# Attention as 64-row head pairs, with scores that telescope over key tiles

## What is computed

```python
h = _layernorm(x) * (1 + ca) + sa
qkv = (h @ W_qkv + b_qkv).reshape(b, l, 16, 192).transpose(0, 2, 1, 3)
Q, K, V = jnp.split(qkv, 3, axis=-1)
scores = einsum('bhqd,bhkd->bhqk', Q, K) / sqrt(64)
out = einsum('bhqk,bhkv->bhqv', softmax(scores), V)
x = x + ga * (out.transpose(0, 2, 1, 3).reshape(b, l, 1024) @ W_fc + b_fc)
```

## Time and profile before

| | |
|---|---|
| median of three runs | 1919.35 us (1916.85 to 1920.01) |
| the profiled execution's own time | 1920.44 us |
| its span, first to last instruction | 1918.7 us |
| mean granted TensorE clock | 0.971 |
| busy: PE, PEld, DVE, ACT, POOL | 1813.9, 991.3, 1313.7, 1051.4, 1169.5 us |
| instructions | 29207 |

### The profile page before, as it was taken

The page is one execution under the profiler, slowest core; times in us unless marked ns, Lnnn a source line. Parts: engine busy times, 40 slices in busy tenths (PEclk is TensorE's granted clock), DMA queues, the critical chain, the costliest instruction groups (busy, mean ns, idle before and its releaser), DMA issues. The chain is left out here.

```text
span 1918.7 us, 29207 instructions
## 1 busy us (share of the span) xinstructions
PE 1813.9 (95%) x7819; PEld 991.3 (52%) x7819; DVE 1313.7 (68%) x2687; ACT 1051.4 (55%) x1944; POOL 1169.5 (61%) x521
## 2 busy tenths in 40 slices
PE   4799999999999999999999999999999999946996
PEld 3444555555555555455555555555555555434886
DVE  5777666666666666666666666666666666467788
ACT  3455555555555555555555555555555555414874
POOL 4466666667666666666766666666667666711124
PEclk8899999999999999999999999999999999956999
DMA  2111111111111111111111111111111111020010
GB/s 84 50 45 50 45 50 47 46 44 50 50 42 41 49 50 50 49 45 43 50 50 50 44 49 48 45 50 47 47 44 50 50 39 40 18 72 22 26 36 28
DMA packets 81217, 87.96 MB, mean 46 GB/s; under 512 B 27773, under 2 KB 50842, under 8 KB 81178
## 3 DMA queue, kind: packets, MB, share of 16 engines
q1 hardware_dynamic: 81024, 87.47, 16.6%
q10 hardware_dynamic: 154, 0.03, 0.0%
HBM read 31.35 MB, written 2.36 MB: 18 GB/s over the span
## 5 line engine op out<-in xcount | busy, mean ns | idle before, releaser
L581 POOL TENSOR_TENSOR ACC<-ACC,PR 128x1024 f32<-128x1024 f32 x382 | 924.6, 2420 | 256.0 <-ACT PR L638 255.1
L666 DVE TENSOR_REDUCE NMH<-ps_mx 128x1 f32<-128x512 f32 x1016 | 693.1, 685 | 491.6 <-PE ps_mx L827 487.1
L638 ACT ACTIVATE PR<-ps_s 128x512 f32<-128x512 f32 x1024 | 556.0, 595 | 617.1 <-PE ps_s L841 612.7
L850 PE MATMUL ps_o<-PR,V 128*64 128x512 f32 x2048 | 548.9, 614 | 0.0
L827 PE MATMUL ps_mx<-KA,QA 128*128 128x512 f32 x1016 | 456.7, 450 | 8.7 <-DVE NMH L666 8.2
L840 PE MATMUL ps_s<-QA,KA 128*128 128x512 f32 x1024 | 408.7, 399 | 0.0
L841 PE MATMUL ps_s<-QB,KB 128*128 128x512 f32 x1024 | 403.4, 394 | 0.0
L827 PEld LDWEIGHTS ps_mx<-KA,QA 128*128 128x128 f32 x1016 | 190.9, 188 | 407.4 <-issue 202.2
L581 POOL TENSOR_TENSOR ACC<-PR 128x1024 f32<-128x1024 f32 x64 | 161.9, 2530 | 278.8 <-ACT PR L638 278.8
L841 PEld LDWEIGHTS ps_s<-QB,KB 128*128 128x128 f32 x1024 | 192.7, 188 | 44.5
L850 PEld LDWEIGHTS ps_o<-PR,V 128*64 128x64 f32 x2048 | 106.9, 135 | 207.2 <-issue 105.0
(11 more groups left out here) (187 smaller groups left out, 1519.8 us busy)
## 6 DMA issues: line engine op xcount, KB each, us to landing
hcur<-hT SPq DMA_DIRECT2D x32, 512.0 KB, 3.6
KA<-KA SPq DMA_DIRECT2D x128, 128.0 KB, 2.3
QB<-QA SPq DMA_DIRECT2D x128, 128.0 KB, 2.2
SUM<-recip_rows SPq DMA_DIRECT2D x128, 128.0 KB, 2.9
Wraw<-in_L_attn_W_qkv SPq DMA_DIRECT2D x32, 192.0 KB, 2.4
x<-in_L_attn_X SPq DMA_DIRECT2D x4, 512.0 KB, 5.3
Wfc<-in_L_attn_W_fc SPq DMA_DIRECT2D x32, 64.0 KB, 1.8
R<-SUM SPq DMA_DIRECT2D x128, 2.0 KB, 1.8
```

What stands on the lines that cost most here:

```text
L581: G.tensor_tensor(ACC[:, ch, :, :], a, PR[:, t, :, :], ALU.add).then_inc(added, 1)
L638: A.activation(PR[:, t, h, :], ps_s[:, h, :], ACT.Exp, scale=SCALE).then_inc(exp_done, 1)
L666: D.tensor_reduce(NMH[:, ch, h, i, kc:kc + 1], banks[:, kc, :], AX, ALU.max, negate=True).then_inc(mx_red, 1)
L850: last = T.matmul(ps_o[half(h), ch, :], V[:, u, t, half(h)], PR[:, t, h, :], start=(t == 0), stop=(t == 7))
```

## The change

The layout: a head keeps its 64 rows. The two heads of a pair lie in the upper and lower 64 partitions of QH, QL (q hi, lo), KH (K hi), and every product of q and K is issued as two, one per head, each on 64 rows of the array and into a bank of its own.

Scores telescope. Key tiles 0 and 1 are started from the row of negative maxima (a product of ones with BQ); from tile 2 on the bank isn't started again: to the scores of tile t - 2 the product with the difference K(t) - K(t - 2) is added. That difference is rounded to DH, its rest kept in DL. So a step has three products per head, or four where the bank starts.

The order: one turn of the loop is a double step d of two key tiles. TensorE does in it: a maximum group, the scores of both steps, a second maximum group, sums (d = 3, 5), PV of the last double step, the row transpose (d = 3, 7), then one projection or output unit. A maximum group is now (chunk, query tile, half of the keys), both heads at once, hi parts alone, one bank of `ps_mx` per head; the next waits until both are reduced. `ps_s` takes four banks (two steps x two heads), `ps_o` and `ps_w` one each.

ScalarE: one exponential of 128 x 1024 per step; K's copy Kraw, its hi part KH and the step DH; q's hi part straight from PSUM with its bias; a copy of `ps_o` into O. VectorE: the step K(t) - K(t - 2) written back into PSUM, DL, QL, both straight from PSUM; NM by one reduction; O times SUM with both in SBUF. SP: the duplicates of K and q are gone. The sums' chain has one double step from sums to reciprocal (d = 3 to 4, 5 to 6) and one to the normalisation (d = 5, 7).

```diff
+        QH = sb("QH", [P, 2, L], F32R)   # also QL, KH, DH, DL; Kraw = sb("Kraw", [P, L])
+        ps_s = psum("ps_s", [P, 2, 2, 512])
         ps_mx = psum("ps_mx", [P, 2, 512])
+        ps_o = psum("ps_o", [P, 512])
+        ps_w = psum("ps_w", [P, 512])
+        LATE = {0: ("k", 1, 0), 1: ("k", 1, 1), 2: ("q", 1, 0), 3: ("q", 1, 1), 4: ("v", 1, 0), 5: ("fc", -1, 1),
+                6: ("v", 1, 1), 7: ("fc", 0, 0)}
+        SUMS = {3: (-1, 1), 5: (0, 0)}
+        RECIP = {4: (-1, 1), 6: (0, 0)}
+        NORM = {5: (-1, 1), 7: (0, 0)}
...
# SP: dup_k and dup_q removed
# ACT
+                if kind == "k":      # early_part
+                    A.activation(Kraw[:, q], ps_w[:, :], ACT.Identity, bias=bias[:, u, 1:2]).then_inc(k_raw, 1)
+                elif kind == "q":
+                    A.activation(QH[:, u, q], ps_w[:, :], ACT.Identity, bias=bias[:, u, 0:1]).then_inc(q_hi, 1)
...
+            def late_part(kind, m, u, ch):      # k only
+                A.activation(KH[:, u, q], Kraw[:, q], ACT.Copy)
+                act.wait_ge(k_step, 2 * m + ch + 1)
+                A.activation(DH[:, u, ch * 512 + new.start:ch * 512 + 512], ps_w[:, new], ACT.Copy).then_inc(k_hi, 1)
...
+                A.activation(PR[:, t, :, :], ps_s[:, t % 2, :, :], ACT.Exp, scale=SCALE).then_inc(exp_done, 1)
+                for d in range(8):      # pair: late_part of the last unit, then
+                    exponentials(n, 2 * d)
+                    exponentials(n, 2 * d + 1)
+                    # copy_o (d = 0, 4), sums, split_w (d = 6), then early_part of this unit
# DVE
+                for h in range(2):      # reduce_max
+                    dve.wait_ge(mx_done, 2 * count + h + 1)
+                    D.tensor_reduce(NMH[:, ch, h, i, kc:kc + 1], ps_mx[:, h, :], AX, ALU.max, negate=True).then_inc(mx_red, 1)
...
+                    D.scalar_tensor_tensor(QL[:, u, q], ps_w[:, :], bias[:, u, 0:1], QH[:, u, q].bitcast(F32),
+                                           op0=ALU.add, op1=ALU.subtract).then_inc(q_lo, 1)
...
+                dve.wait_ge(recip_in, 32 * (2 * m + ch + 1))
+                dve.wait_ge(o_copied, 2 * m + ch + 1)
+                D.tensor_tensor(O[:, ch, :], O[:, ch, :], SUM[:, ch, :], ALU.mult).then_inc(o_norm, 1)
...
+                for d in range(8):      # pair
+                    if d % 4 == 0 and (d or has(n - 1)):
+                        mask_rows(n, d // 4)
+                    x = late_at(n, d - 1)
...
+                        early_part(*x)
+                        reduce_max(*group(n, u, k), 16 * n + k)
+                        late_part(*x)
+                        invert(n + RECIP[d][0], RECIP[d][1])
+                        normalise(n + NORM[d][0], NORM[d][1])
+                        reduce_max(*group(n, u, k + 1), 16 * n + k + 1)
# PE
+                wait(pe, mx_red, 2 * count)      # maxima
+                for h in range(2):
+                    T.matmul(ps_mx[:, h, :], QH[half(h), u, q:q + P], KH[half(h), u, kc * 512:(kc + 1) * 512],
+                             start=True, stop=True).then_inc(mx_done, 1)
...
+                hi = KH if t < 2 else DH      # scores
+                if t < 2:
+                    for h in range(2):
+                        T.matmul(ps_s[:, t, h, :], one_r[half(h), :], BQ[half(h), ch, :], start=True, stop=False,
+                for h in range(2):
+                    T.matmul(ps_s[:, t % 2, h, :], hi[half(h), u, k], QH[half(h), u, q], start=False, stop=False,
+                for h in range(2):
+                    T.matmul(ps_s[:, t % 2, h, :], DL[half(h), u, k], QH[half(h), u, q], start=False, stop=False,
+                for h in range(2):
+                    last = T.matmul(ps_s[:, t % 2, h, :], hi[half(h), u, k], QL[half(h), u, q], start=False, stop=True,
...
+                for d in range(8):      # pair
+                        maxima(*group(n, u, k), 16 * n + k)
+                    scores(n, u, 2 * d)
+                    scores(n, u, 2 * d + 1)
+                        maxima(*group(n, u, k + 1), 16 * n + k + 1)
+                        sums(n + SUMS[d][0], SUMS[d][1])
+                        times_v(n, u, 2 * d - 2)
+                        times_v(n, u, 2 * d - 1)
+                        rows(m, ch)
+                        unit(x[0], x[1], parity(u, LATE[d][1]), x[2])
```

More of the change, by code:

```diff
@@ L614, in unit @@
                 elif kind == "v":
                     act.wait_ge(v_proj, 2 * m + ch + 1)
[L616 to L620, removed]
+                    A.activation(flat(V[:, u, 4 * ch:4 * ch + 4, :]), ps_w[:, :], ACT.Copy).then_inc(v_copied, 1)
@@ L676, in unit @@
-                    for h in range(2):
-                        last = D.tensor_tensor(KB[half(h), u, h, q], raw[half(h), ch, :], KA[half(h), u, h, q].bitcast(F32), ALU.subtract)
-                    last.then_inc(k_lo, 1)
+                    dve.wait_ge(k_raw, 2 * m + ch + 1)
+                    new = slice(256 - 256 * ch, 512)
+                    D.scalar_tensor_tensor(ps_w[:, new], ps_w[:, new], bias[:, u, 1:2], Kraw[:, 256 * ch:256 + 512 * ch],
+                                           op0=ALU.add, op1=ALU.subtract).then_inc(k_step, 1)
@@ L773, in _, with unit @@
             T = nc.tensor
-            def unit(kind, m, u, ch, ps_w):
-                q = slice(ch * 512, ch * 512 + 512)
+            def unit(kind, m, u, ch):
                 if kind in "qk":
@@ new lines, in first, with previous @@
+                maxima(*group(0, 0, 4), 4)
+                maxima(*group(0, 0, 5), 5)
+                freed(("v", 0, 0))
+                unit("v", 0, 0, 1)
+                for k in (6, 7, 8):
+                    maxima(*group(0, 0, k), k)
+                pe.wait_ge(mx_red, 18)
+                rows(0, 0)
+            def previous(n, d, sums_now):
+                if not sums_now and d in SUMS and has(n + SUMS[d][0]):
+                    return ("sums", n + SUMS[d][0], SUMS[d][1])
+                k = d - 1
+                while True:
+                    x = late_at(n, k) if k >= 0 or has(n - 1) else None
+                    if x:
+                        return x
+                    e = k % 8
+                    j = n + k // 8
+                    if e in SUMS and has(j) and has(j + SUMS[e][0]):
+                        return ("sums", j + SUMS[e][0], SUMS[e][1])
+                    if k < -8:
+                        return None
+                    k -= 1
@@ L887, in pair @@
                     if x:
[L889 to L890 removed]
+                        before = previous(n, d, False)
                         if before:
[L892 to L895 removed]
```

440 lines of the change are left out of this document (192 added, 248 removed).

## The result

The changed kernel takes 1834.04 us (median of four runs, 1833.84 to 1838.18), the kernel before 1919.68 (four runs): a ratio of 0.956 [0.955, 0.958], so 86 us are gone. The profiled execution of after is the one of 1838.18 us, with a span of 1836.5.

What follows compares the result with a forecast made beforehand. TensorE's instruction stream was taken to bound the attention loop. At 48.0 us a pair, 32 pairs take 1536 against 1611 us (-75); the start adds 6.5, giving about 1850 us, range 1700 to 1960.

Steps and rivals of the forecast that it cites:

- the likeliest case: Attention loop: VectorE's reductions of the first maximum group delay the second; 1800 to 1890 us, chance 0.55.
- Couples side by side, 0.235 us: TensorE: a couple's two 64-row products overlap, taking 0.235 us; bounds 0.233 (full overlap) and 0.466 (none).
- The second rival: TensorE: row tiles do not run side by side, 0.466 us a couple, 57.2 us a pair, 2145 us; chance 0.10.
- The change into the row form: TensorE: switching the array into 64-row tiles costs 0.09 us, like a change between two column forms.
- The chain, M - S by double step: From first to second maximum group: projection's end, ScalarE's copy, VectorE's share, two reductions; 1.88 to 2.91 us, sum 19.4 a pair.
- Pair: One head pair of the attention loop: eight double steps, 47.6 us in all, against 50.35 before.
- The lock: VectorE's normalisation, both inputs in SBUF, may wait out a GpSimd addition: 0 to 2.4 us each, 0.4 a pair taken.
- The start: Before the loop: K's longer chain and nine maximum groups on two banks; main loop at about 76 instead of 69.5 us, +6.5.
- TensorE alone: Attention loop: TensorE's own work without waits for other engines, 41.5 us a pair, 8.9 less than before.
- the first rival: Attention loop: only TensorE's work binds, 41.5 to 45 us a pair, 1644 to 1755 us; chance 0.13.
- The exponential and GpSimd's additions off the path: ScalarE's 1024-column exponential, at most 1.09 us, and GpSimd's 14 additions, 34 us a pair, stay hidden.
- the fifth rival: Attention loop: pauses lower TensorE's clock to 0.90, costing some 3 us a pair, ending near 1945 us; chance 0.04.

Runs made afterwards that it cites:

- the first edit: Changed kernel with VectorE's two reductions of the first maximum group moved ahead of its share of the last projection: 1769.95 us, ratio 0.925.
- the two fastest versions that leave nothing out: Changed kernel with reductions first and normalisation on GpSimd, 1739.77 us; that plus the first maximum group ahead of the unit in six double steps, 1735.76 us.

## Why the prediction was right

The forecast was 1850 and the likeliest case holds: the reductions bind the second group. Point by point.

- **Couples side by side, 0.235 us.** Measured 0.23; and 0.46 where they can't be. The second rival priced that case at 2145 with the maxima serial too; with the scores alone serial it is 2053. The Trainium skill, TensorEngine Tiling (Array Packing), section Key Properties, says that tiles load and multiply in parallel; the trace agrees, by 0.23 against 0.46.
- **The change into the row form.** Taken like that of two column forms, 0.09 us. The distance into it agrees (903.63 to 903.96 is 0.33 us, against 0.23 without a change), but the next one is 0.33 too (903.96 to 904.29), where the sum put 0.235: the change costs 0.2 in the two together.
- **The chain, M - S by double step.** Forecast 2.22, 2.58, 2.85, 2.85, 2.91, 1.88, 2.22, 1.88; measured 2.26, 2.57, 2.84, 2.82, 2.64, 1.88, 2.16, 1.88: a sum of 19.05 where 19.4 stood. The low part of q lasts 0.75 us and not 0.69, but the reduction starts 0.67 behind its start (904.78 to 905.45). Only d = 4 is off by more than 0.1, by 0.27: its first group waits for VectorE's mask behind the row transpose and comes 0.51 us behind the last projection product instead of 0.33, which shortens the distance; the chain itself is that of a q. In d = 0 the match is luck: no wait stands ahead of its second group (936.55), and the 2.26 us are TensorE's own nine couples, for which 2.1 stood, below a chain of 2.22.
- **Pair.** 47.6 forecast without the lock, 47.4 measured.
- **The lock, mis-sized.** 0.4 us a pair were set down for it, 12.8 in all. In after the normalisation of the loop is blocked twice in 61 rows (2.02 and 2.06 us; 0.683 is the median): nearly nothing. It lies in wait, though: 1.73 us in the median when the normalisation comes later, up to 2.89 when the rhythm is faster. The Trainium skill, SBUF — State Buffer, section Who interferes with whom, says that a VectorE instruction with two SBUF inputs contends with a GpSimd instruction that reads SBUF; the trace agrees, in 2.89 us beside an addition that started 0.02 us before.
- **The start.** 6.5 us forecast, 8.28 measured. The forecast took only the longer chain. The granted clock in it is lower too: 0.50 in 50 to 60 us, with TensorE busy 5.38 of 10 us, where the kernel before had 0.90 with 5.68. What of the 1.8 us that makes was not tried. The window of before:

```profile
50.00:60.00 10.00, 5.68 (x20) 3.29 (x20) 7.39 (x12) 6.73 (x13) 3.82 (x4) 0.90 0.49 136
```

- **TensorE alone.** 41.5 us a pair were added up; with the waits nearly gone it is 42.7. About 0.8 of the 1.2 us is the distance from each first group to its scores, 0.33 instead of 0.235 eight times a pair. So the first rival's lower end (1644) was out of reach; 1683 is what the runs show, with half the reductions' work left out.
- **The exponential and GpSimd's additions off the path.** So they are: two exponentials change nothing.

The sum: -75 forecast for the loop; without the lock's 12.8 and with 0.2 less a pair it is -94, and the loop measured -92 (a few pairs are longer than 47.4). With a start 8.28 us longer and 1.8 us more behind the loop, for which nothing was set down, that is -82 in span, where -68.5 was forecast. The median lies 4 us lower still, since the profiled execution is the slowest of the four.

That the reductions bind is shown by two independent edits (order, length) and by both together; that the normalisation on VectorE, by its lock and its late DMA together, costs the first edit most of the 30 us, by the version that has it on GpSimd. What makes only some pairs of that edit collide, and how the remaining waits of the two fastest versions that leave nothing out could be had back, was not tried; nor was what the order alone (PV for two steps at once) and the missing duplicates of q and K are worth.

## What to carry to other kernels

Taking work from the engine that is the bound can move the bound to the longest chain that must end before this engine's next step, and that chain may go through engines that are busy for 64% of the time or less, as here: write it out from the projection's end to the released bank, in each engine's written order, before adding up busy times. Then put work that releases the bound engine ahead of work that only must be done by the next step. And an instruction with two inputs in SBUF on VectorE has a price that depends on where GpSimd is at that moment: a faster rhythm changes it, so look at its longest and median rows again after every change.

## What the runs showed of the hardware

- A small minimum that had two SBUF inputs took 0.79 us in most rows; as one reduction over a single input it takes 0.17 in all 64, 33 of which start inside an addition of GpSimd. The low parts of the weights (L624, two SBUF inputs, 128 x 128) still meet an addition: 651 ns in the median, 277 at the least.

```profile
L624 DVE TENSOR_TENSOR Wlo<-Wraw,Whi x60: 277/651/1069, 116.2 to 1497.3; 128x128 fp32r<-128x128 f32 x60
```

- A wait in which TensorE stands 0.3 to 1 us at a time, 7% of the loop, leaves its granted clock at 1.00 in 900 to 1000 us; the fifth rival (0.90 in the loop) did not come. In the start the clock is 0.50 in 50 to 60 us, where it is busy 5.38 of 10 us.
